# Moving the rough scores' rows ahead of the other rows, with a semaphore of their own, in a gated cross-attention kernel

## The reference, cut to what matters

```
x = x + tanh(g_xattn) * attention(layernorm(x), ctx)       # 16 heads of 16 dims
    q = ln(x) @ Wq ; k = ctx @ Wk ; v = ctx @ Wv
    attn = softmax(q k^T / 4) ; out = (attn @ v) @ Wo
x = x + tanh(g_ffn) * ffn(layernorm(x))                    # 256 -> 1024 -> 256, gelu
    the two weights are made ternary first
```

## Time and profile before

| | us |
|---|---|
| median of 3 runs | 1601.36 (1598.82 to 1603.03) |
| the profiled execution | 1602.56 |
| its span | 1600.6 |

### The profile page before, as it was taken

How to read it: one execution, slowest core, us unless ns; L and a number is a source line. 1 busy time by engine, 2 the same in 40 slices (tenths; PEclk the granted TensorE clock), 3 DMA queues, 4 the chain that set the end, 5 groups by cost and what they waited for, 6 DMA issues and landing times.

```text
span 1600.6 us, 52630 instructions
## 1 busy us (share of the span) xinstructions
PE 1351.8 (84%) x18085; PEld 1005.7 (63%) x18085; DVE 1262.9 (79%) x2998; ACT 975.4 (61%) x1683; POOL 839.2 (52%) x1233
## 2 busy tenths in 40 slices
PE   2788888888888888888888888868999999999998
PEld 2566666666666666666666666645666666666665
DVE  6687887778777877787788777778888888888886
ACT  3566666666666666666666667636555555555553
POOL 6477767777777777777777777631111111111110
PEclk9799999999999999999999999968999999999999
DMA  2655555565656565646565655420010101010101
GB/s 75 109 93 95 105 94 94 94 109 88 101 98 103 83 106 95 105 83 104 99 102 87 99 102 84 72 69 17 27 39 26 39 26 39 26 39 26 39 26 53
DMA packets 155729, 118.99 MB, mean 74 GB/s; under 512 B 22321, under 2 KB 155441, under 8 KB 155697
## 3 DMA queue, kind: packets, MB, share of 16 engines
q1 hardware_dynamic: 155696, 118.56, 41.2%
HBM read 32.53 MB, written 16.78 MB: 31 GB/s over the span
## 4 chain that ended last, share of the span: by engine, by line
PE 34%; DVE 21%; DMA 19%; issue 12%; SPq 8%; ACT 4%; DVEq 1%; POOL 0%; ACTq 0%; POOLq 0%
DMA qk_rows<-qk 13%; PE bank L1219 12%; DMA qk_rows<-smaxT 6%; DVE smax L898 6%; PE bank L1248 5%; PE bank L1249 5%; SPq L240 5%; PE bank L381 3%; DVE y L1206 2%; DVE stats L784 2%; PE bank L461 2%; DVE qk L855 2%; SPq L237 2%; PE bank L340 2%; DVE smax L906 2%
## 5 line engine op out<-in xcount | busy, mean ns | idle before, releaser
L1059 POOL TENSOR_TENSOR prob<-prob 128x512 f16<-128x512 f32 x512 | 533.9, 1043 | 258.7 <-ACT prob L654 250.8
L654 ACT ACTIVATE prob<-bank,masks 128x512 f32<-128x512 f32 x512 | 352.0, 688 | 277.4 <-PE bank L418 271.5
L898 DVE TENSOR_REDUCE smax<-bank 128x4 f32<-128x512 f32 x512 | 346.2, 682 | 149.5 <-PE bank L381 149.4
L381 PE MATMUL bank<-qk_rows 64*128 64x128 f16 x2048 | 206.2, 223 | 137.7 <-DMA qk_rows<-qk 70.3
L1230 ACT ACTIVATE hid<-bank,b_sb 128x512 f32<-128x512 f32 x256 | 175.9, 688 | 211.3 <-PE bank L1219 205.0
L1313 POOL TENSOR_TENSOR xres<-xres,b2g 128x1024 f32 (+1 forms) x32 | 75.3, 2354 | 430.6 <-ACT yln L1183 413.5
L1235 DVE TENSOR_TENSOR hidl<-hid 128x512 f16<-128x512 f32 x256 | 225.6, 881 | 80.6 <-ACT hid L1230 79.6
L1219 PE MATMUL bank<-y,w1T 128*128 128x512 f16 x1024 | 264.6, 381 | 28.8 <-DVE y L1206 27.6
L381 PEld LDWEIGHTS bank<-qk_rows 64*128 64x128 f16 x2048 | 117.7, 96 | 223.5 <-DMA qk_rows<-qk 86.0
L1248 PE MATMUL bank<-w2T,hid 128*128 128x256 f16 x1024 | 237.4, 273 | 0.6 <-ACT w2T L1159 0.6
L1249 PE MATMUL bank<-w2T,hidl 128*128 128x256 f16 x1024 | 237.3, 273 | 0.0
(11 more groups left out here) (116 smaller groups left out, 2605.1 us busy)
## 6 DMA issues: line engine op xcount, KB each, us to landing
qk_rows<-qk SPq DMA_DIRECT2D x384, 128.0 KB, 4.0
xres<-in_x_dram SPq DMA_DIRECT2D x32, 512.0 KB, 3.5
qk_rows<-qk SPq DMA_DIRECT2D x256, 64.0 KB, 3.3
out_dram<-ystage SPq DMA_DIRECT2D x32, 512.0 KB, 3.0
ctx_sb<-in_ctx_dram SPq DMA_DIRECT2D x64, 192.0 KB, 4.0
qk_rows<-smaxT SPq DMA_DIRECT2D x128, 16.0 KB
w_raw<-in_L_ffn_W_dram SPq DMA_DIRECT2D x2, 1024.0 KB, 6.8
prob<-in_L_xattn_Wq_dram SPq DMA_DIRECT2D x1, 256.0 KB, 4.4
```

The costliest lines, as they stand in the source:

```text
L381: return pe.matmul(sm_bank[u % 2][:, c * S:(c + 1) * S], q, k, start=True, stop=True)
L654: act.activation(prob[u][:], st_bank[u % 2][:], ACT.Exp, bias=0.0, scale=masks[g.parity][:, 2 + b:3 + b]).then_inc(exp_done, 1)
L898: dve.tensor_reduce(smax[:, b, u * UH:(u + 1) * UH], sm_bank[u % 2][:].rearrange("p (h j) -> p h j", h=UH), AX.X, ALU.max).then_inc(max_ta ...
L1059: pool.tensor_tensor(prob[u][:].bitcast(F16)[:, 0::2], prob[u][:], prob[u][:].bitcast(BF16)[:, 1::2], ALU.subtract).then_inc(prob_split, 1)
```

## The change

SP moves the rough rows of both batches of group g+2 in one call each (`move_rough`, one 128 KB transfer a batch) as soon as `q_high` and `k_high` stand, and they count on a semaphore `rough_moved`, one for each parity and batch. The other four transfers of a batch (`move_qk`) count on `qk_moved`, also by parity and batch. `rough_free` waits for `rough_moved`; `scores` waits for `qk_moved` at u = 0. In SP's list the maxima of (g, 1) now stand ahead of q and k of (g+1, 1), the rough rows of g+2 ahead of x and of the maxima of (g+1, 0), and q of (g+2, 0) goes behind those maxima with k. Before ACT writes the high q of a later group it waits for both semaphores of both batches. The number of transfers and bytes is the same.

```diff
-    MOVES = 5
+    MOVES = 4
-        def move_q(sp, g, b, split, free):
+        def move_rough(queue, g, b, high):
+
+            queue.wait_ge(q_high, high)
+            queue.wait_ge(k_high, high)
+            queue.dma_start(qk_rows[g.parity][RB:RB + HD, b].rearrange("d j i m s -> d j (i m s)"),
+                         qk16[g.parity][:, b, KH:QH + 1].rearrange("p i m s -> p (i m s)")).then_inc(rough_moved[g.parity][b], 16)
+
+        def move_qk(sp, g, b, split, free):
             if free is not None:
 
                 sp.wait_ge(scored, free)
 
             sp.wait_ge(q_split, split)
-            sp.dma_start(rows_of(g, b, slice(0, HD), 0), qk16[g.parity][:, b, QH].rearrange("p m s -> p (m s)")
-                         ).then_inc(qk_moved[b], 16)
-
-        def move_k(sp, g, b, split):
-
             sp.wait_ge(k_split, split)
-            sp.dma_start(rows_of(g, b, slice(0, HD), 1), qk16[g.parity][:, b, KH].rearrange("p m s -> p (m s)")
-                         ).then_inc(qk_moved[b], 16)
-            for r, i in ((HD, QL), (2 * HD, QH), (RB, KH)):
+            for i, half in ((0, QH), (1, KH)):
+                sp.dma_start(rows_of(g, b, slice(0, HD), i), qk16[g.parity][:, b, half].rearrange("p m s -> p (m s)")
+                             ).then_inc(qk_moved[g.parity][b], 16)
+            for r, i in ((HD, QL), (2 * HD, QH)):
...
             if left >= 1:
-                move_q(sp, g.after(1), 1, split1, scored_before)
-                move_k(sp, g.after(1), 1, split1)
-            move_max(sp, g, 1, max_b1)
+                move_qk(sp, g.after(1), 1, split1, scored_before)
             if left >= 2:
-                move_q(sp, g.after(2), 0, split2, scored_b0)
+                for b in range(2):
+                    move_rough(sp, g.after(2), b, split2)
             if g.parity == 0 and left >= 6:
...
             if left >= 2:
-                move_k(sp, g.after(2), 0, split2)
+                move_qk(sp, g.after(2), 0, split2, scored_b0)
...
-                pe.wait_ge(qk_moved[b], 16 * MOVES * (g.n + 1))
+                pe.wait_ge(rough_moved[g.parity][b], 16 * (g.half + 1))
...
             if u == 0:
 
+                pe.wait_ge(qk_moved[g.parity][b], 16 * MOVES * (g.half + 1))
                 pe.wait_ge(max_moved[b], 16 * (g.n + 1))
```

More of the change, by code:

```diff
@@ L191, in bass_gated_cross_attention_ternary_ffn @@
         v_made, v_high, v_split = sem("v_made"), sem("v_high"), sem("v_split")
-        qk_moved = [sem(f"qk_moved{b}") for b in range(2)]
+        rough_moved = [[sem(f"rough_moved{p}{b}") for b in range(2)] for p in range(2)]
+        qk_moved = [[sem(f"qk_moved{p}{b}") for b in range(2)] for p in range(2)]
         weights_high, weights_split = sem("weights_high"), sem("weights_split")
@@ L230, in move_q @@
             sp.wait_ge(q_split, split)
-            sp.dma_start(rows_of(g, b, slice(0, HD), 0), qk16[g.parity][:, b, QH].rearrange("p m s -> p (m s)")
-                         ).then_inc(qk_moved[b], 16)
-        def move_k(sp, g, b, split):
             sp.wait_ge(k_split, split)
-            sp.dma_start(rows_of(g, b, slice(0, HD), 1), qk16[g.parity][:, b, KH].rearrange("p m s -> p (m s)")
-                         ).then_inc(qk_moved[b], 16)
-            for r, i in ((HD, QL), (2 * HD, QH), (RB, KH)):
+            for i, half in ((0, QH), (1, KH)):
+                sp.dma_start(rows_of(g, b, slice(0, HD), i), qk16[g.parity][:, b, half].rearrange("p m s -> p (m s)")
+                             ).then_inc(qk_moved[g.parity][b], 16)
+            for r, i in ((HD, QL), (2 * HD, QH)):
                 sp.dma_start(qk_rows[g.parity][r:r + HD, b].rearrange("d j i m s -> d j (i m s)"),
-                             qk16[g.parity][:, b, i:i + 2].rearrange("p i m s -> p (i m s)")).then_inc(qk_moved[b], 16)
+                             qk16[g.parity][:, b, i:i + 2].rearrange("p i m s -> p (i m s)")).then_inc(qk_moved[g.parity][b], 16)
         def move_max(sp, g, b, copied):
@@ L275, in sp_group @@
                 sp.wait_ge(rough_scored, UNITS + 1)
+            move_max(sp, g, 1, max_b1)
             if left >= 1:
-                move_q(sp, g.after(1), 1, split1, scored_before)
-                move_k(sp, g.after(1), 1, split1)
-            move_max(sp, g, 1, max_b1)
+                move_qk(sp, g.after(1), 1, split1, scored_before)
             if left >= 2:
-                move_q(sp, g.after(2), 0, split2, scored_b0)
+                for b in range(2):
+                    move_rough(sp, g.after(2), b, split2)
             if g.parity == 0 and left >= 6:
@@ L617, in high_q @@
                 for b in range(2):
-                    act.wait_ge(qk_moved[b], 16 * MOVES * (g.n - 1))
+                    act.wait_ge(rough_moved[g.parity][b], 16 * g.half)
+                    act.wait_ge(qk_moved[g.parity][b], 16 * MOVES * g.half)
             act.activation(halves_of(g, QH), pj_halves, ACT.Identity, bias=0.0,
@@ L1343, in _ @@
             for b in range(2):
-                move_q(sp, Group(0, 0), b, 1, None)
-                move_k(sp, Group(0, 0), b, 1)
+                move_rough(sp, Group(0, 0), b, 1)
+            for b in range(2):
+                move_qk(sp, Group(0, 0), b, 1, None)
             sp.wait_ge(ln_ready, 2)
@@ L1352, in _ @@
             sp.wait_ge(k_rows_set, 4)
-            move_q(sp, Group(0, 1), 0, 2, None)
-            move_k(sp, Group(0, 1), 0, 2)
+            for b in range(2):
+                move_rough(sp, Group(0, 1), b, 2)
+            move_qk(sp, Group(0, 1), 0, 2, None)
             over_groups(sp, sp_group, 3)
```

## The result

The changed kernel takes 1661.07 us (median of 4 runs, 1655.42 to 1663.35) against 1602.19 (4 runs) for the kernel before on the same chip: a ratio of 1.036, with a 95% interval of 1.034 to 1.038. It is 3.6% slower. I had forecast 1549, with a range up to 1576: wrong, and on the wrong side.

A forecast was written before the change was run, and what follows sets the result against it. The chain of waits, q and k rows first, was taken to bound the kernel. Gains of 44, 5, 4 and 5 us less 5 for the clock made 53 off 1602.6: 1549.6, so 1549 for the median, range 1506 to 1576.

The forecast's parts named there:

- I take 1.8: New wait for the maxima at step 0 behind even groups that load x: 1.8 us, bounds 0 and 2.5.
- the clock -5: Slow output projections no longer hidden by the wait at step 1, four in odd groups: 5 us lost in all.
- The start: Start-up: gain at step 1 of group 0 against the new wait at its end, taken as nothing.
- the last groups: Groups 61 and 62, whose wait before step 1 was put at 2.45 us: 5 us more gained.
- C: Slower than before: the rough pair delays the maxima of (g+1, 0) in odd groups too; 1624 to 1671 us, chance 0.07.
- Rival B: Only the wait at step 1 shrinks, the rest returns on DVE or the clock; 1581 us, chance 0.11.
- Rival A: x does not hold the maxima: wait of 0.2 us instead of 1.8, 1503 us, chance 0.18.

The follow-up runs named there:

- rough_sem: The kernel before, with only a separate semaphore for the rough rows, which go first of the four transfers behind k's low half: 1593.3 us, ratio 0.994.
- max1_behind: `x_behind` with the maxima of (g, 1) put back behind the four transfers of (g+1, 1): 1606.9 us, ratio 1.004 to the kernel before.
- x_behind: The changed kernel, with the load of x moved from ahead of to behind the maxima of (g+1, 0) on SP: 1508.0 us, ratio 0.942.
- filler: The changed kernel, with 22 unused matmuls on PE at the end of each even group, ahead of the wait for the maxima: 1576.6 us, ratio 0.985.
- split_pair: The changed kernel, with one rough transfer ahead of the maxima of (g+1, 0), the other behind, then x: 1478.7 us, ratio 0.924.
- hold_qk: The changed kernel, where SP waits for the maxima of (g+1, 0) to land before issuing q and k of (g+2, 0): 1563.8 us, ratio 0.976.
- x_early: The changed kernel, with the load of x issued ahead of the rough pair on SP: 1595.0 us, ratio 0.995.

## Why the prediction was wrong

**The parts that gain were right.** The rough rows leave with the high halves, and the wait at step 1 is gone. With the maxima of (g, 1) ahead of four transfers step 4 waits for no transfer either; that this part is needed is shown by `rough_sem` and `max1_behind`. An odd group with the full clock takes 14.27 to 14.3 us in `x_behind` and `filler`, where I took 14.4. An even group without a wait takes 13.7 in `split_pair`, where I took 13.9.

**"I take 1.8" was mis-sized.** The mechanism and its place were right, and its issue times within 0.3 us: 1.6 to 2.1 us of new wait at step 0 behind the groups that load x. It was 2.65 us, above even the bound of 2.5. I had counted the bytes ahead of the maxima and not the four transfers issued 0.76 us behind them; `hold_qk` takes these away and the wait is 1.42, below the 1.6. The even group came to 16.65 us instead of 15.7: 28 x 0.95 = 27 us.

**The step that failed is "the clock -5".** I had seen that the clock falls behind waits at steps 4 and 6, and had counted nine such falls as they stood. I had written that PE's gaps change their place, with 20 us for 15 more, and then put that at nothing. But the change does not only move gaps. Before, each group had one wait of some 1.4 us at step 1 and one of about 1.0 at step 4; now a pair of groups has one of 2.65 in one piece. That one is followed by the lower level in the trace in 26 of 28 odd groups, and twice in 25 of them. The typical odd group came to 17.47 us instead of 14.4. Over all 28, with the few that kept the clock, that is 79 us; against the odd groups of `filler`, 14.28 us in the mean, it is 83. So the term that I had put at 5 us, and at 20 for 15 more falls, was about 80.

The forecast and the measurement differ by 112 us. The two terms give 27 + 79 = 106, of which 5 were in the sum. The start, taken as nothing, cost 6 (group 0 loads x too, and the wait behind it is 4.10 us), and the last groups gave back 7.5 where I had counted 12, so 4 more are missing. That makes 111. (In the sum only group 61 had the wait of 2.45 us before step 1; that of group 62 was 3.61 us, so this term was 1 us short.) Of the rivals, C had the sign and the size (1624 to 1671), but the wrong mechanism: it asked for maxima held up in odd groups too. In the odd groups they were not late; the time went to the clock. Rival B had a clock that falls more often, but priced it at 10 us. Rival A was wrong: x does hold the maxima, as `x_behind` shows. The ceiling of the Trainium skill's page "DMA: Bandwidth & Descriptors", under "Where 436 GB/s comes from", was not reached by these transfers: in the slices of 0.3 us from 606 to 612 the changed kernel moved at most 208 GB/s while the rough pair passed and 358 while x did.

## What to carry to other kernels

In a queue of transfers, look for the small one that an engine waits for. In this kernel both what large transfers stood ahead of it and what was issued right behind it were paid on the critical path; moving one load of 512 KB by one place was worth 153 us of 1661 here. When a change leaves TensorE with one longer wait in place of several short ones, price the clock too: look at the granted clock of the stretch behind each long gap, and test by filling the gap with useless matmuls.

## What the runs showed that I had not expected

The 16 KB of maxima need 2.2 us when nothing is close to them (the median for those of (g+1, 0) in the kernel before), 3.91 with 256 KB ahead and x 0.85 us behind, 5.38 with 768 KB ahead and 384 KB close behind, but 4.15 if nothing follows closely. That transfers issued later delay the landing of an earlier one was new to me.

So was how little idle time can come before a fall of the clock, and that the length of the wait alone does not decide it. Behind the waits of the changed kernel, mostly of 2.65 us, it fell in 26 of 28 odd groups, but not behind one of 2.29 and the one of 2.57 us shown above. Behind those of 1.8 to 2.4 us in `x_early` it fell in 12 of 28, and behind those of 1.4 to 1.6 us in `hold_qk` in 12 of 28 as well. The kernel before had a wait of some 1.4 us and one of about 1.0 in nearly every group, and a fall in 9 of 56. What else decides is not shown by these runs.

Part of the loss is that one fall lengthens the next wait. In the traces of the changed kernel, `x_early` and `hold_qk`, PE idled 0.6 to 0.8 us at the transpose of the maxima in the odd groups that kept the clock, and 1.4 to 1.5 in all but two of those that had lost it at their start. Whether this idle time in turn brings the second fall is open: a second fall came in 25 of 26 such groups in the changed kernel, but in 7 of 12 in `x_early` and 3 of 12 in `hold_qk`. `filler` removed both, and the second was not tried alone.
